# Attention in an attention + mixture-of-experts layer: heads in pairs on row halves, masks of both passes ahead of the scores

## The chip, the cores and the metric

The kernel runs on one core of a Trainium2 chip. The metric is the device time of one execution in microseconds (us). The kernel before takes 1405.36 us, the median of three runs (1402.96 to 1407.62).

## The reference

```python
x = x + attn(layernorm(x))                  # x is 8 x 512 x 256, f32
x = x + experts(layernorm(x))
# attn: q, k, v = x @ W.T + b, 16 heads of 16; rotary embedding on q and k;
#       causal softmax(q k^T / 4) v; then @ Wo.T + bo
# experts: 8 experts, the 2 best of a router for each token, at most 153 tokens
#       per expert and batch; silu((t Wf + bf) * (t Wg + bg)) Wp + bp, weighted sum
```

## The kernel before, in words

The program has two phases, `attention_phase` and `expert_phase`. The diff touches the first. Each of the five engines has its own instruction stream, written out by hand with semaphores between them.

**Slots.** Attention runs over 8 batches (`b`), 4 groups of 4 heads (`g`), and 8 slots (`u`) in each group, on all engines in the same order. A slot is written (g,u). In slot u, TensorE computes two heads' scores twice. The *first pass* (`pass1`, L392) has queries on the partitions, query tile i = u // 2 and 256 to 512 keys; VectorE takes the maximum over the keys (L794). The maxima are transposed (piece M, L465), negated (ScalarE, L584) and sent by DMA as one more row of the query stack (L337). The *second pass* (`pass2`, L412) works on the group of two groups earlier. It has keys on the partitions, key tile j, and 512, 384, 256, 256 queries; the extra row subtracts the maximum, and ScalarE takes the exponential (L569, L577) into `probs`. Then `pv` (L437) multiplies with `v_sb` (L445), its four heads in four column strips of the array; it is called four times per group, at u = 3, 5, 7 and the next group's u = 1.

**Operands.** q and k are split in two parts each (`hilo`), so that fp32r products keep precision. They go to DRAM (L318) and come back (`load_stack`, L320 to 331) as stacks of 4 x 16 rows for a head: all four products of the parts in one matmul of 65 or 66 rows (`qst`, `kst`). The causal mask is added by a matmul with an identity and a bf16 mask: L401/L405 ahead of the first pass's scores, L422/L432 ahead of the second's. Masks and scores of a pass stand together.

**Pieces.** The rest of the work of three batches is cut into pieces, at most one per slot (`PIECES`, L235): for batch b+1 X (transposed normalised input), Q (0 to 3, the projections of q and k, L475) and V (L477); for b A (transposed PV output, L469) and M; for b-1 T and O (output projection, L486 to 491); for b-2 H, L, R, F (router and ranks). All use the PSUM bank `misc`, PV its own; the first pass has four banks, the second two. `last_piece` finds which eviction has to be over before the bank is used again.

**The other engines.** ScalarE evicts Q (L605), X, T, H, PV (L593). VectorE does the reductions, the rotation (shuffle L811, product with sin L812, sum L817), both normalisations (L697), the copy of v (`v_sb`, L822), v's eviction (L774), the residual (L781), attention's scaling (L757, L761) and routing (L703 to L749). POOL does the product with cos (L935), the split of the rotated values (L947, L950), two Newton chains for 1/sqrt (L908 to L916) and the scatter of tokens (L964). SP issues the DMAs. A loop over b = 2 to 6 has the steady code; b = 0, 1, 7, 8 are written out, and the last pieces lie in slots of the experts' first block (`LATE_SLOTS`, L1069).

```python
def pv(t, bt, g, j):                                   # L437
    wait(pe, exp_done, tiles2(t, 2 * j + 1, 1))
...
if u in (3, 5, 7) and (not isinstance(b, int) or 0 <= s - 2 <= 31):
    pv(s - 2, b - (g < 2), (g - 2) % 4, (u - 3) // 2)  # L535
```

Of the kernel before, what the change touches and what calls it, by code (L numbers as in the profile page):

```python
# [6 lines left out]
F32 = mybir.dt.float32  # L7
# [8 lines left out]
P = 128  # L16
BATCH, T, C = 8, 512, 256
TT = T // P
# [5 lines left out]
ZROW = NP * DH  # L24
MROW = ZROW + 1
ROWS = MROW + 1
SLOTS = 8
# [7 lines left out]
MASKED = -1e30  # L35
# [10 lines left out]
CAUSAL = IDENT + P  # L46
# [57 lines left out]
def attention_phase(nc, d, rt, block, outer):  # L104

    ctx = ExitStack()
    with ctx:
# [3 lines left out]
        def sem(name):  # L120
# [11 lines left out]
        ident_bf = sb("ident_bf", [P, P], BF16)  # L132
# [10 lines left out]
        bv_all = sb("bv_all", [P, C])  # L143
# [10 lines left out]
        x1 = late.take("x1", [P, TT, C])  # L154

# [4 lines left out]
        stats1 = sb("stats1", [P, TT, 6])  # L160
        mv1 = sb("mv1", [P, TT, 2])
        rs1 = sb("rs1", [P, 3, TT])
# [8 lines left out]
        qst = sb("qst", [ROWS, NG, GH, T], F32R)  # L171
        kst = sb("kst", [ROWS, NG, GH, T], F32R)
        mx = sb("mx", [P, 2, TT, GH])
        negmax = sb("negmax", [GH, 2, T], F32R)
        probs = sb("probs", [P, 2, GH, T])
        rden = kept.take("rden", [P, TT, GH])
        stats2 = kept.take("stats2", [P, TT, 6])
        mv2 = kept.take("mv2", [P, TT, 2])
        rs2 = kept.take("rs2", [P, 3, TT])
# [19 lines left out]
        pvb = ps[:, 6, :]  # L199
        misc = ps[:, 7, :]  # L200
# [23 lines left out]
        sin_done, rope_done, oh_done, dlt_done, put_done = (sem("sin_done"), sem("rope_done"), sem("oh_done"),  # L224
                                                            sem("dlt_done"), sem("put_done"))
        rs1_done, rs2_done = sem("rs1_done"), sem("rs2_done")
        cos_done, hilo_done, xr_done = sem("cos_done"), sem("hilo_done"), sem("xr_done")
        dve_step, newton1, newton2 = sem("dve_step"), sem("newton1"), sem("newton2")
        hilo_half = sem("hilo_half")
        sp_passed, dve_passed, pool_passed = sem("sp_passed"), sem("dve_passed"), sem("pool_passed")  # L230
# [3 lines left out]

        PIECES = {  # L235
# [7 lines left out]
        }  # L243
        Q_AT = ((1, 1), (1, 4), (1, 6), (2, 1))
        FIRST = [at for at in sorted(PIECES) if PIECES[at][0] in "XQV"]

        def bank_of(b, g, u):
            return ps[:, FIRST.index((g, u)), :] if isinstance(b, int) and b == -1 else misc

        def piece_there(b, g, kind):  # L250
            s = 4 * b + g
            return {
                "M": there(s, 1, 32) if isinstance(b, int) else True,
                "A": there(s, 3, 34) if isinstance(b, int) else True,
# [5 lines left out]
        def freed(b, g, kind, n):  # L260
            return {
                "M": (negmax_out, 4 * b + g),
                "A": (at_out, 4 * b + g - 2),
# [11 lines left out]
        def last_piece(b, g, u):  # L275

            if isinstance(b, int) and b == -1:
                return None
            keys = sorted(PIECES)
            at = keys.index((g, u))  # L280
            for back in range(1, 2 * len(keys)):
# [4 lines left out]
                if (not isinstance(bb, int) or bb >= -1) and piece_there(bb, gg, kind):  # L286
                    if isinstance(bb, int) and bb == -1 and kind not in "XQV":
                        continue
                    return freed(bb, gg, kind, n)
# [1340 lines left out]
```

## Time and profile before

| | us |
|---|---|
| median of three runs | 1405.36 (1402.96 to 1407.62) |
| the profiled execution, its own time | 1391.76 |
| its span | 1389.9 |
| TensorE busy | 1238.5 |
| VectorE busy | 729.6 |
| POOL busy | 697.0 |
| ScalarE busy | 496.3 |
| mean granted TensorE clock | 0.943 |

In the rows below PE is TensorE's matmuls, PEld its weight loads, DVE is VectorE, ACT ScalarE, POOL GpSimd, SP the engine that issues most DMAs; "q" behind a name is an engine's queue. `L401` is line 401. A busy matmul includes its latency; the distance between the starts of two matmuls says what one costs. The granted clock is the share of TensorE's full clock that the chip let it have.

### The profile page before, as it was taken

The page shows a single profiled execution, that of the slowest core. Times are in us where ns is not written, and L with a number is a line of the kernel's source. Part 1 is how long each engine was busy: PE and PEld are TensorE (multiplying, and loading weights), DVE is VectorE, ACT ScalarE, POOL GpSimd, SP SyncE. Part 2 cuts the span into 40 slices and gives each one's busy share as a digit, 9 for nine tenths or more (in the row PEclk, how much of TensorE's full clock was granted, in tenths as well). Part 3 has the DMA queues.
Part 4 walks back from the last instruction along what each step waited for, and adds up shares of the span by engine and source line. Part 5 has one row for each costly group of instructions (what it writes and reads, how often), then busy time and mean ns, then how long its engine had stood idle before and what let it go on. Part 6 is the DMA issues. An engine that isn't in the chain of part 4 may idle for free.

```text
span 1389.9 us, 25801 instructions
## 1 busy us (share of the span) xinstructions
PE 1238.5 (89%) x8360; PEld 1023.6 (74%) x8360; DVE 729.6 (52%) x1512; ACT 496.3 (36%) x988; POOL 697.0 (50%) x984
## 2 busy tenths in 40 slices
PE   3699999999898989988899999999999999997830
PEld 3465656566565656548899999999999999997730
DVE  5777776858676767556333343343333433333336
ACT  2145444535353535454223332333233332332100
POOL 4334243343425251267755665576656764634445
PEclk9699999999999999999999999999999999998865
DMA  5766545444434453432312211131122112102247
GB/s 138 216 208 193 177 115 144 109 132 103 138 93 139 100 149 93 137 124 60 96 62 91 70 62 62 64 98 54 66 78 87 54 58 70 64 28 72 69 131 249
DMA packets 82333, 147.86 MB, mean 106 GB/s; under 512 B 9263, under 2 KB 59832, under 8 KB 78142
## 3 DMA queue, kind: packets, MB, share of 16 engines
q1 hardware_dynamic: 64576, 111.37, 28.1%
q0 software_dynamic: 7936, 26.60, 5.6%
q10 hardware_dynamic: 9728, 8.67, 2.0%
q8 instruction: 56, 0.92, 0.3%
q14 instruction: 37, 0.30, 0.1%
HBM read 93.05 MB, written 53.61 MB: 106 GB/s over the span
## 4 chain that ended last, share of the span: by engine, by line
PE 45%; another core or an unknown queue 2%; DVE 1%; POOL 1%; issue 1%; DMA 0%; DVEq 0%; ACT 0%; POOLq 0%; ACTq 0%
PE ps L77 44%; PE ps L1264 1%; DVE raw L1427 1%; POOL wg_hi L1544 1%; POOL wf_hi L1544 0%; DMA wg_hi<-slot_outputs,slot_all 0%; DVE al L1417 0%; DVEq L1454 0%; DVE ah L1408 0%; POOLq L1572 0%; ACT hid L1349 0%; ACT fc L1360 0%; DVE xl L1332 0%; DVE gated L1455 0%
## 5 line engine op out<-in xcount | busy, mean ns | idle before, releaser
L1491 POOL TENSOR_TENSOR al<-hid,ah 128x384 fp32r<-128x384 f32 (+1 forms) x176 | 187.4, 1065 | 232.9 <-DVE ah L1408 232.9
L1360 ACT ACTIVATE fc<-ps,b_fc 128x384 f32<-128x384 f32 (+1 forms) x192 | 115.5, 602 | 482.4 <-PE ps L77 441.2
L1455 DVE SCALAR_TENSOR_TENSOR gated<-ps,b_gate,fc 128x384 f32<-128x384 f32 (+1 forms) x192 | 123.4, 643 | 268.1 <-PE ps L77 220.2
L794 DVE TENSOR_REDUCE mx<-ps 128x2 f32<-128x256 f32 (+3 forms) x256 | 206.6, 818 | 67.1 <-PE ps L408 56.5
L577 ACT ACTIVATE probs<-ps 128x512 f32<-128x512 f32 (+1 forms) x256 | 125.6, 541 | 73.8 <-PE ps L434 72.0
L408 PE MATMUL ps<-kst,qst 65*128 65x256 f32 (+2 forms) x512 | 151.7, 380 | 0.0
L1442 DVE TENSOR_TENSOR o_sb<-ps,b_proj 128x256 f32<-128x256 f32 x80 | 33.9, 424 | 179.0 <-PE ps L77 175.1
L569 ACT ACTIVATE probs<-ps 128x256 f32<-128x256 f32 (+1 forms) x128 | 62.6, 490 | 164.4 <-PE ps L425 150.0
L445 PE MATMUL ps<-probs,v_sb 128*32 128x512 f32 (+3 forms) x1024 | 98.8, 459 | 14.2 <-DVE v_sb L822 14.0
L77 PE MATMUL ps<-xh,wg_hi 128*128 128x384 f32 (+1 forms) x384 | 104.4, 353 | 5.0 <-DVE gated L1455 4.2
L935 POOL TENSOR_TENSOR rope_c<-qk_b,rope_table 128x512 f32<-128x512 f32 x32 | 42.7, 1333 | 128.9 <-ACT qk_b L605 128.7
L77 PE MATMUL ps<-wp_hi,ah 128*128 128x256 f32 (+1 forms) x640 | 89.7, 283 | 17.0 <-DVE al L1417 17.0
L434 PE MATMUL ps<-qst,kst 66*128 66x512 f32 (+1 forms) x256 | 103.9, 457 | 0.0
L77 PE MATMUL ps<-xh,wg_lo 128*128 128x384 f32 (+1 forms) x384 | 103.8, 352 | 0.0
L77 PE MATMUL ps<-xl,wg_hi 128*128 128x384 f32 (+1 forms) x384 | 103.8, 352 | 0.0
L1349 ACT ACTIVATE hid<-gated 128x384 f32<-128x384 f32 (+1 forms) x192 | 102.8, 535 | 1.4 <-DVE gated L1455 0.8
L77 PE MATMUL ps<-xh,wf 128*128 128x384 f32 (+1 forms) x384 | 90.6, 358 | 7.4 <-DVE xl L1332 7.3
L77 PEld LDWEIGHTS ps<-wp_hi,ah 128*128 128x128 f32 (+1 forms) x640 | 83.3, 186 | 17.9 <-issue 17.6
L77 PE MATMUL ps<-wp_hi,al 128*128 128x256 f32 (+1 forms) x640 | 88.9, 281 | 0.0
L77 PE MATMUL ps<-wp_lo,ah 128*128 128x256 f32 (+1 forms) x640 | 88.6, 281 | 0.0
L1408 DVE CAST ah<-hid 128x384 fp32r<-128x384 f32 (+1 forms) x192 | 87.7, 457 | 0.8 <-ACT hid L1349 0.8
L408 PEld LDWEIGHTS ps<-kst,qst 65*128 65x128 f32 x512 | 83.1, 204 | 2.5 <-issue 0.3
(181 smaller groups left out, 2577.5 us busy)
## 6 DMA issues: line engine op xcount, KB each, us to landing
qk_parts<-hilo SPq DMA_DIRECT2D x32, 512.0 KB, 3.1
qst<-qk_parts SPq DMA_DIRECT2D x64, 256.0 KB, 4.8
kst<-qk_parts SPq DMA_DIRECT2D x64, 256.0 KB, 5.2
slot_tokens<-zeros POOLq DMA_DIRECT2D x12, 816.0 KB, 5.6
rows<-slot_tokens SPq DMA_DIRECT2D x24, 384.0 KB, 3.7
slot_outputs<-o_sb SPq DMA_DIRECT2D x72, 128.0 KB
raw<-in_wf SPq DMA_DIRECT2D x8, 1024.0 KB, 6.1
raw<-in_wg SPq DMA_DIRECT2D x8, 1024.0 KB, 7.6
```

The source lines that it names most:

```text
L77: last = nc.tensor.matmul(out, w, x, start=(i == 0), stop=(i == len(terms) - 1))
L408: last = mm(bank, qst[0:MROW, g, h, bass.ts(i, P)], kst[0:MROW, g, h, 0:width], start=False, stop=True, skip_group_check=True)
L434: mm(ps[:, S2 + hh, 0:T - q0], kst[0:ROWS, g, h, bass.ts(j, P)], qst[0:ROWS, g, h, q0:T], start=False, stop=True, skip_group_check=True).t ...
L445: last = mm(pvb[32 * h:32 * h + 32, P * j:T], v_sb[:, j, GH * g + h, :], probs[:, j % 2, h, P * j:T], start=(j == 0), stop=(j == TT - 1))
L569: A(probs[:, j % 2, 2 * pr:2 * pr + 2, P * j:T], ps[:, S2 + pr, :].rearrange("p (h q) -> p h q", h=2)[:, :, P * j - q0:T - q0], ACT.Exp, s ...
L577: A(probs[:, j % 2, 2 * pr + hh, P * j:T], ps[:, S2 + hh, P * j - q0:T - q0], ACT.Exp, scale=float(DH) ** -0.5).then_inc(exp_done, 1)
L794: V.reduce_max(mx[:, g % 2, i, 2 * pr:2 * pr + 2], both[:, :, 0:P * (i + 1)], AXX)\
L1349: A(hid[:, hc % 2, 0:width], gated[:, hc % 2, 0:width], ACT.Silu).then_inc(hid_done, 1)
L1360: A(fc[:, hc % 2, 0:width], ps[:, FC + hc % 2, 0:width], ACT.Identity, bias=b_fc[:, e, hc:hc + 1]).then_inc(fc_out, 1)
L1408: V.tensor_copy(ah[:, (8 * n + hc) % RING, 0:width], hid[:, hc % 2, 0:width]).then_inc(ah_done, 1)
L1455: V.scalar_tensor_tensor(gated[:, hc % 2, 0:width], ps[:, GATE + hc % 2, 0:width], b_gate[:, e, hc:hc + 1], fc[:, hc % 2, 0:width], ALU.ad ...
L1491: G.tensor_tensor(al[:, at, 0:width], hid[:, hc % 2, 0:width], ah[:, at, 0:width].bitcast(F32), ALU.subtract).then_inc(al_done, 1)
```

## The change

**Row halves.** The stacks keep three products of the parts instead of four: 48 rows and one for the maximum, 49 in all. Heads lie in pairs: one head of a pair in partitions 0 to 48, the other in 64 to 112. Each mask becomes a matmul of 64 rows: `pick_bf` has two entries per row, one of them 2^-88, and the mask has values for two columns of positions, so that 64 rows make 128. Each head of a pair has its own bank, in both passes.

**Order in a slot.** The masks of the first pass, the masks of the second pass, the scores of the first, the scores of the second, the pieces. The second pass's masks wait for the exponentials of the slot before. There is one exponential per slot, for both heads (8 semaphore counts per group instead of 12).

**PV.** One piece "P" at u = 1, for all key tiles of the group before the previous one; `probs` keeps a whole group, packed.

**Pieces.** They use two banks, LOW and HIGH (6 and 7), and a slot can have two: X,X at (0,0); O,O at (3,0). Q moves to (0,4), (0,6), (1,0), (1,5), V to (3,4), (3,5), M to u = 2; L, R, F and the routing move later, the scatter to (2,6), (2,7), (3,0), (3,1).

**Work moved.** POOL now multiplies by cos and sin (`cos_sin`), normalises (both), copies v, and has one Newton chain for both norms. VectorE shuffles the sin product and adds (`rotate`). ScalarE makes the large part of the split (`large_part`) and evicts v; POOL makes the small part. v's bias is folded into the output bias, once, in the prologue. The input of batch b+2 is loaded and normalised in b, one batch earlier. A stack load is eight DMAs instead of four, the row of maxima two instead of one. Batch 6 is written out too. The experts' code is the same, but for wait counts.

```diff
-            def pass2(t, g, u):
-                if u >= PAIRED:
-                    wait(pe, exp_done, tiles2(t, u, 0) - 2)
-                    mm(bank[:, :, P * j - q0:P * (j + 1) - q0], ident_bf[:], later_bf[:].unsqueeze(1).to_broadcast([P, 2, P]),
-                        start=True, stop=False, skip_group_check=True)
...
+            rows_of = [slice(HALF * hh, HALF * (hh + 1)) for hh in range(2)]
+            def first_masks(b, g, u):
+                if u == 0:
+                    wait(pe, ld_stack[g], 128 * (b + 1))
+                wait(pe, red_done, 8 * (4 * b + g) + u - 1)
+                for hh, half in enumerate(rows_of):
+                    mm(first_bank(u, hh)[:, bass.ts(u // 2, P)], pick_bf[half, 0], causal_bf[half],
+                       start=True, stop=False, skip_group_check=True)
+            def first_scores(g, u):
+                for hh in range(2):
+                    rows = slice(HALF * hh, HALF * hh + MROW)
+                    last = mm(first_bank(u, hh)[:, 0:width], qst[rows, g, pr, bass.ts(i, P)], kst[rows, g, pr, 0:width],
+                              start=False, stop=True, skip_group_check=True)
+                last.then_inc(p1_done, 1)
+            def second_masks(t, u):
+                if u == 0:
+                    wait(pe, ld_max, 32 * (t + 1))
+                wait(pe, exp_done, TILES2 * t + u)
...
+                elif kind == "P":
+                    wait(pe, exp_done, TILES2 * (s - 2))
+                    for j in range(TT):
+                        for h in range(GH):
+                            last = mm(misc[32 * h:32 * h + 32, P * j:T], v_sb[:, j, GH * group + h, :],
+                                      probs[:, (g + 1) % 2, h, PROB_AT[j]:PROB_AT[j + 1]], start=(j == 0), stop=(j == TT - 1))
...
+                for g, u in before_late(b):
+                    s = 4 * b + g
+                    if there(b, 0, 7):
+                        first_masks(b, g, u)
+                    if second_there(s):
+                        second_masks(s - 2, u)
+                    if there(b, 0, 7):
+                        first_scores(g, u)
+                    if second_there(s):
+                        second_scores((g - 2) % 4, u)
+                    pieces(b, g, u)
...
+            def exps(t, g, u):
+                wait(act, p2_done, TILES2 * t + u + 1)
+                A(probs[:, g % 2, 2 * pr:2 * pr + 2, PROB_AT[j]:PROB_AT[j + 1]], ps[:, S2:S2 + 2, P * j - q0:T - q0], ACT.Exp,
+                  scale=float(DH) ** -0.5).then_inc(exp_done, 1)
...
+            def large_part(b, n):
+                wait(act, rope_done, 4 * b + 4 + n + 1)
+                wait(act, st_hilo[n // 2], 32 * (b + 1))
+                A(hilo[:, n, 0, :], rope_c[:, n % 2, :], ACT.Copy).then_inc(hilo_half, 1)
+            LARGE_AT = ((1, 0), (1, 2), (1, 4), (2, 3))
...
+            def rotate(chain, b, n):
+                wait_apart(dve, cs_done, 4 * b + 4 + n + 1, dve_passed)
+                chain(V.stream_shuffle(qk_b[:, n % 2, :], rope_s[:, n % 2, :], SWAP))
+                V.tensor_tensor(rope_c[:, n % 2, :], rope_c[:, n % 2, :], qk_b[:, n % 2, :], ALU.add).then_inc(rope_done, 1)
+            ROTATE_AT = ((0, 7), (1, 1), (1, 3), (2, 2))
```

## Rows read from the trace of the kernel before

**Rows 1.** The page, busy time, share of the span and instructions of each engine.
```profile
PE 1238.5 (89%) x8360; PEld 1023.6 (74%) x8360; DVE 729.6 (52%) x1512; ACT 496.3 (36%) x988; POOL 697.0 (50%) x984
```

**Rows 2.** Windows by batch: us, then busy us (instructions) of each engine; last clock, DMA.
```profile
39.80:96.20 56.40, 50.83 (x298) 33.63 (x298) 40.88 (x67) 17.69 (x34) 19.76 (x32) 0.80 0.71 218
162.60:235.30 72.70, 67.69 (x502) 43.77 (x499) 52.52 (x114) 33.34 (x68) 28.36 (x46) 0.95 0.50 136
...
383.20:457.10 73.90, 68.02 (x501) 44.16 (x497) 52.53 (x114) 33.34 (x68) 29.08 (x49) 0.95 0.45 120
...
531.40:592.50 61.10, 57.94 (x445) 36.13 (x441) 36.62 (x82) 29.89 (x62) 14.09 (x26) 0.94 0.45 121
...
626.00:1389.90 763.90, 685.01 (x4415) 664.34 (x4413) 299.94 (x633) 222.78 (x437) 455.05 (x600) 0.95 0.24 79
```

**Rows 3.** Timeline of PE, slot (1,2) of a batch: start, us, instruction.
```profile
403.36 0.28 PE L401 MATMUL ps<-causal_bf,ident_bf 128*128 128x256 bf16 x1
...
404.02 0.23 PE L432 MATMUL ps<-later_bf,ident_bf 128*128 128x128 bf16 x1
404.06 0.42 PE L434 MATMUL ps<-qst,kst 66*128 66x384 f32 x1
404.32 0.28 PE L401 MATMUL ps<-causal_bf,ident_bf 128*128 128x256 bf16 x1
```

**Rows 4.** Timeline of PE, a PV step and a Q projection; groups of lines, both O.
```profile
405.57 1.07 PE L445 MATMUL ps<-probs,v_sb 128*32 128x512 f32 x8
406.57 0.65 PE L451 MATMUL ps<-consts_sb,pv_sb 128*128 128x128 f32 x4
...
412.52 0.62 PE L77 MATMUL ps<-xnT_hi,wq_hi 128*128 128x512 f32 x2
...
413.92 0.28 PE L405 MATMUL ps<-causal_bf,ident_bf 128*128 128x128 bf16 x2
...
L490 PE MATMUL ps<-wo,attnT 128*128 128x256 f32 x16 | 4.0, 392 | 0.0
```

**Rows 5.** Groups of ACT, one batch: busy us, mean ns | idle before, releaser.
```profile
L577 ACT ACTIVATE probs<-ps 128x512 f32<-128x512 f32 x16 | 8.7, 593 | 6.0 <-PE ps L434 5.9
L577 ACT ACTIVATE probs<-ps 128x384 f32<-128x384 f32 x16 | 7.0, 490 | 4.2 <-PE ps L434 4.0
```

**Rows 6.** Groups of DVE, the same batch.
```profile
L794 DVE TENSOR_REDUCE mx<-ps 128x2 f32<-128x1024 f32 x9 | 10.9, 1219 | 3.4 <-remote 1.5 <-issue 1.2 <-PE ps L408 0.7
...
L811 DVE STREAM_SHUFFLE rope_s<-qk_b 128x512 f32<-128x512 f32 x4 | 3.0, 740 | 0.0
...
L741 DVE TENSOR_SCALAR over<-pos 128x8 f32<-128x8 f32 x1 | 1.8, 1776 | 0.0
```

**Rows 7.** Groups of POOL, the same batch.
```profile
L964 POOL DMA_INDIRECT slot_tokens<-hn,put_at x8 | 8.1, 1007 | 3.9 <-issue 2.0 <-DVE put_at L747 1.9
...
L935 POOL TENSOR_TENSOR rope_c<-qk_b,rope_table 128x512 f32<-128x512 f32 x4 | 5.1, 1276 | 17.0 <-ACT qk_b L605 17.0
```

**Rows 8.** Waits of PE in that batch (us, times, longest); PE's first slot, timeline.
```profile
PE ps L445 <- DVE v_sb L822: 2.5, 1, 2.5
...
39.82 0.37 PE L401 MATMUL ps<-causal_bf,ident_bf 128*128 128x256 bf16 x1 [11.98 <-DMA kst<-qk_parts]
```

**Rows 9.** Windows of 4 us: PE, PEld, DVE, ACT, POOL busy, granted clock, DMA.
```profile
40.00:44.00 4.00, 2.79 (x15) 2.16 (x14) 3.02 (x11) 0.00 (x0) 0.81 (x4) 0.50 1.07 275
...
604.00:608.00 4.00, 3.26 (x23) 1.52 (x22) 3.66 (x13) 3.60 (x8) 1.54 (x1) 1.00 0.89 303
...
423.00:427.00 4.00, 2.15 (x10) 0.52 (x11) 2.30 (x4) 0.00 (x0) 3.07 (x3) 0.70 0.25 90
...
403.00:407.00 4.00, 4.00 (x29) 2.14 (x28) 2.99 (x7) 2.41 (x6) 1.27 (x1) 1.00 0.69 162
```

**Rows 10.** Timeline of PE, the A pieces of two groups in the last pass.
```profile
598.75 0.66 PE L451 MATMUL ps<-consts_sb,pv_sb 128*128 128x128 f32 x4
...
609.11 0.66 PE L451 MATMUL ps<-consts_sb,pv_sb 128*128 128x128 f32 x4
```

More of the change, by code:

```diff
@@ L380, in _ @@
             body(1)
-            with sp.Fori(2, 7) as b:
+            with sp.Fori(2, 6) as b:
                 body(b)
-            body(7)
-            body(8)
+            for b in range(6, 9):
+                body(b)
             rt["late_slot"]["sp"] = body_slot
@@ L547, in _ @@
+            pe.wait_ge(bv_ready, 1)
+            for c in range(CK):
+                last = mm(bank_of(-1, "X", 1)[:, 0:C], bv_wide[:, c, :], wo[:, c, :], start=(c == 0), stop=(c == CK - 1))
+            last.then_inc(bo_done, 1)
             pe.wait_ge(made, 5)
             pe.wait_ge(ld_ones, 32)
+            pe.wait_ge(v_out, 2)
+            pe.wait_ge(bo_out, 1)
             body(0)
             body(1)
-            with pe.Fori(2, 7) as b:
+            with pe.Fori(2, 6) as b:
                 body(b)
-            body(7)
@@ L554, in _ @@
-            body(8)
-            rt["late_slot"]["pe"] = piece
+            for b in range(6, 9):
+                body(b)
+            rt["late_slot"]["pe"] = pieces
         @block.scalar
@@ L776, in body_slot @@
-                if (g, u) in ((3, 2), (3, 3)) and piece_there(b, g, "O"):
-                    n = u - 2
-                    wait(dve, o_done, 2 * b - 2 + n + 1)
+                    for n in range(CK):
+                        wait(dve, xT_out, 2 * b + 2 + n + 1)
+                        V.tensor_tensor(xnT[1][:, n, :], bank_of(b, "X", n), xnT[0][:, n, :].bitcast(F32), ALU.subtract)\
+                            .then_inc(xl_out, 1)
+                if (g, u) == (3, 1) and there(b, 1, 8):
                     wait(dve, xr_done, b)
@@ L833, in body @@
+                if (g, u) == (3, 2) and there(b, 1, 8):
+                    wait(dve, o_out, 2 * b)
+                    layer_stats(chain, x1, 1, mv2_done)
             def body(b):
@@ new lines, in rsqrt, with normalise, normalise_input @@
+                    step(G.tensor_tensor(y, y, a, ALU.mult))
+            def normalise(dst, src, which, done):
+                for k in range(TT):
+                    ins = G.tensor_scalar(dst[:, k, :], src[:, k, :], mv[:, which, k, 0:1], rs[:, 1, which, k:k + 1],
+                                          ALU.subtract, ALU.mult)
+                ins.then_inc(done, 1)
+            def normalise_input(b):
+                wait_apart(pool, xT_done, 2 * b, pool_passed)
+                normalise(xn, x_in, 0, xn_done)
@@ L955, in body_slot @@
                         .then_inc(xr_done, 1)
+                if (g, u) == (2, 3) and there(b, 0, 7):
+                    wait(pool, v_out, 2 * (b + 1))
+                    wait_apart(pool, pv_done, 4 * b, pool_passed)
+                    G.tensor_copy(v_sb[:, :, :, 0:DH], v_next[:].rearrange("p t (h r) -> p t h r", h=HEADS)).then_inc(v_moved, 1)
                 if (g, u) in SCATTER_AT and there(b, 2, 9):
@@ L992, in _ @@
             pool.wait_ge(st_zero, 16 * FILLS)
-            with pool.Fori(2, 7) as b:
+            with pool.Fori(2, 6) as b:
                 body(b)
-            body(7)
-            body(8)
+            for b in range(6, 9):
+                body(b)
             rt["late_slot"]["pool"] = body_slot
@@ L1619 @@
         "consts": constants(),
-        "rows": np.stack([np.zeros(NG * GH * T, np.float32), np.ones(NG * GH * T, np.float32)]),
+        "ones": np.ones((1, NG * PAIRS * T), np.float32),
     }
```

608 lines of the change are left out of this document (280 added, 328 removed), and 7 rows, old and new, of the table PIECES.

## The prediction

> **What bounds the kernel now.** I read the page first, for the stages [rows 1]: TensorE is busy 89% of the span, VectorE 52%, POOL 50%, ScalarE 36%. The change touches only the attention phase, so the windows by batch come next [rows 2]. A batch in the loop takes 72.7 us at its start and 73.9 in the middle, with TensorE busy 68.0 and VectorE 52.5. The last full batch, which prepares no successor, takes 61.1. After 626 us only experts are left, some 764 us that the diff leaves alone.
>
> The timeline of TensorE inside one batch says what a slot costs [rows 3]. A slot without a piece runs from 403.36 to 404.32: 0.96 us for 256+512 columns of the first pass and 2 x (128+384) of the second. The granted clock is 1.00 there, the 2.4 GHz level (403 to 407 has it throughout [rows 9]), at which 1792 columns are 0.75 us; the other 0.21 is loading of weights and hand-overs. So the plain slot is TensorE's own work. Thirty-two of them are 31 us. The pieces, by their starts [rows 4]: 1.00 us for a PV step of 512 columns (2.5 for the 1280 of a group), 1.40 for a Q projection, 2.0 for each half of O (4.0 busy for both); V has Q's columns. 4 x 2.5 + 4 x 1.4 + 2 x 1.5 + 2 x 2.0 = 22.6 us, and 17 short ones at some 0.5 make 31. That is 62 of 74 us. Most of the other 12 is stalls in group 2, as the wait for v_sb (2.5 us) [rows 8], and what follows them at the half clock, as 423 to 427 with 0.70 [rows 9].
>
> **The change, step by step.**
>
> *Masks and scores on row halves.* Two heads now lie in partitions 0-63 and 64-127, and the matmuls of each pair name different halves and different banks. If a pair streams together, a slot's columns fall from 1792 to 128+128+256+384 = 896, 0.37 us. Loads stay, eight for seven; what they and the hand-overs cost is the 0.21 us of the plain slot [rows 3], and I take 0.3 for more waits between changes of weights. The slot is 0.7 us of TensorE work in place of 0.96. The trace shows no row halves; it shows the other direction, PV's four heads in column strips, 8 matmuls of 512 columns in 1.07 us, where 0.21 us each in turn would be 1.7 at the least [rows 4]. That is the nearest row and I take full overlap; no overlap is the other end.
>
> Row halves alternate with the full array wherever a slot has a piece. The PV step now starts 0.3 us or so after the last scores and the next work starts about 0.1 after its stream; I take 0.1 us for a change of shape, with 0 and 0.2 as bounds. The Trainium skill (TensorEngine Tiling (Array Packing), Key Properties) says that different tiles run in parallel and also that a change of tiling mode drains TensorE. By that rule alone 23 slots with pieces, entered and left, would be charged; with 0.2 us for each such slot it is 4.6 us a batch, against 16 PV calls in shape changes before.
>
> *The new loop.* Exp of a pair is now one activation over two banks, and the second pass's masks wait for the exp of the slot before; behind that wait on TensorE are this slot's first scores, so VectorE waits too. ScalarE's exps cost 490 and 593 ns for 384 and 512 elements, 0.80 ns an element more [rows 5]. Pairs have 1024, 768, 512, 256: 1.00, 0.80, 0.59, 0.39 us. From the second mask's load to the end of its score is 0.46 us (404.02 to 404.48) [rows 3]; the first scores in between add 0.15, two hand-overs 0.2. So the loop is exp + 0.8: 1.8, 1.6, 1.4, 1.2 us for the four row blocks, twice each: 12.0 us a group, 48 a batch. That is above TensorE's 0.7. The old slot let the second head's matmul run beside the first head's exp.
>
> *Pieces fill the loop.* A piece runs while the exp does, so a slot lasts the larger of the loop and 0.8 + piece. PV is one piece for 1280 columns: 1280/512 x 1.00 = 2.5 us (bounds 2.3, its streams, and 2.7, the sum of the four steps now). Its slot is 3.3, 1.5 over the loop, four times: 6.0. Four Q (2.2 us slots) add 3.0, two V 1.6, the two O together (0.8 + 4.0) 3.0. Transposes and the router's pieces are within the loop. 48 + 13.6 = 61.6 us, about what it is now without stalls.
>
> *VectorE, ScalarE, POOL.* VectorE loses the sine product, both normalisations, the move of v and v's eviction. It keeps the reduction, 1.22 us in slots 6 and 7 [rows 6], as long as those slots. A rotation (0.74 for its shuffle, about as much for the sum [rows 6]) sits behind a reduction, and ScalarE's large part waits for it, one slot later, ahead of that slot's exp. The rotation of slot (0,7) ends 1.5 us into (1,0); the exp is late by some 1 us. The same at (1,4) and (2,3): 3.3 us a batch. In group 2, slots 4 to 7, VectorE has some 0.7 of attention output, reductions of 2 x 0.9 + 2 x 1.22, and some 4 of routing (one step alone is 1.78) [rows 6]: 9 us in 5.3 us of slots. Two banks and the long slot (3,0) behind it take up part; I take 2.5 us of stall. The old stalls on v_sb and attnT lose their causes, as the move is POOL's at (2,3) and PV of that group is read only in the next group.
> POOL gains 4 sine products at 1.28 [rows 7], eight normalisations (no more than 0.64 each, half a product's elements) and the v copy, and loses 4 conversions and half of the Newton steps: 29 us [rows 2] become about 38 of 68. Its scatters (8.1 us and gaps of 3.9 [rows 7]) start at (2,6) and end near (3,3); the Newton chain and the normalisation follow and end some 1.5 us ahead of the X piece at (0,0). I charge 1 us. A full batch is 61.6 + 3.3 + 2.5 + 1 = 68.4 us.
>
> *DMA.* A stack load is eight transfers instead of four, with 48 rows per head for 64. Per group it has eight slots, over 12 us, to land; hidden, except for the first: body 0 starts on kst, after a wait of 11.98 us [rows 8]. There the four more transfers, POOL's normalisation and the later rotation all count; I take a quarter of that wait, +3 us (bounds 0 and 6).
>
> *The ends.* Body 7: 61.1 -> 58.5 (loop, P, O and the routing stall remain). Bodies 0 and 1 took 56.4 and 66.4 (96.2 to 162.6) [rows 2]; I give them 4.4 each. Body 8 has no first pass; its groups took 10.4 us each (598.75 to 609.11 [rows 10]), and the loop (exp + 0.65) with the single PV piece makes them 12.4: +4.
>
> Sum: 5 x (73.9 - 68.4) = 27.5, + 2.6, + 8.8, - 4, - 3: **32 us saved.** The profiled execution took 1391.8 us for a span of 1389.9; the three runs shown have a median of 1405.4, 1% above it, and I subtract from the median: **1373 us**.
>
> **The rivals.**
> *A, the stalls are not there* (0.20). If VectorE keeps ahead, so that rotations and routing hide, a batch is 61 to 63 us: 5 x 12 + 8 for body 7 + 12 - 7 = 73 us saved, **1332**. For it: the LARGE_AT slots leave one to two slots to each rotation. Against it: reductions as long as the slots.
> *B, the clock falls* (0.11). The loop leaves TensorE waiting in a third of the batch. Where the granted clock is 0.50, work doubles. At 40 to 44 us TensorE, with first passes alone, was busy 2.79 of 4 us and stayed at 0.50, the 1.2 GHz level; at 604 to 608 it was busy 3.26 of 4 with second passes and pieces, and had 1.00 [rows 9]. The second is like the new slots, so this is unlikely. Its place is slots (1,6) to (2,0) and (2,4) to (2,7), and what follows them. If the mean granted clock of a batch falls from 0.95 to about 0.80, that is 40% of the time at half; of 55 us of TensorE work 14 to 20 more, half of it beside waits: +8 us a batch, more than 5.5. Then **1413**, slower. It decides once the mean is under 0.85.
> *C, row halves do not overlap* (0.06). Then a slot has 1664 to 1792 columns again, the loop grows by 0.35 to 0.4: +12 a batch, 80 us, and 1373 + 12 x 7.5 is **1463**. Against it: the column strips of rows 4.
> *D, one more queue* (0.06): POOL's chain misses the X piece by 4 us a batch, or ScalarE's evictions push each exp: the gain is about 30 less, **1402**.
>
> **How the numbers follow.** The forecast has 0.57. About 0.3% (4 us) is what a measurement of this kernel can tell from no change. Faster: 0.57 + 0.20 and a bit of D and B, 0.79. Same: 0.06. Slower: the rest of B and C, 0.15. The unknown costs (overlap of loads 0.1 x 32, shape changes 0 to 4.6, PV 0.2 x 4 per batch) are +-4 us a batch, +-25 in all. The range reaches from A's 1332 to the edge of no change, 1330 to 1404; B's and C's slower ends and some of A's lower side are the 0.2 left out.
>
> **What would show it.** Rows of a first pair of score matmuls with starts a few ns apart and 0.35 us or less from the first mask to the second mask's load; plain slots of 1.2 to 1.8 us, ended by exp; PV in one group of 32 matmuls near 2.5 us; a batch of 66 to 70 us between two v copies; VectorE near 65% of a batch; ScalarE idle ahead of hilo behind rope_c in (1,0), (1,4), (2,3). Wrong would be score pairs with starts 0.1 us or more apart (C), a mean clock under 0.85 in the middle batches (B), or TensorE waiting at X for xn (D).

## The result, and the profile of the changed kernel

Four runs of the changed kernel have a median of 1522.4 us (1511.8 to 1526.2), four of the kernel before 1404.2 (1400.9 to 1407.6): a ratio of **1.083**, 95% interval 1.077 to 1.089. The forecast was 1373 us. The kernel became 8.3% slower, and the time lies above every case that was written down. Some executions of a kernel are over 1.5% longer than its fastest; ratios leave them out and medians do not, so a ratio can differ a little from the quotient of two medians.

The page of the changed kernel, busy time and share of each engine, then the granted clock in 40 slices:

```profile
span 1524.3 us, 25626 instructions
...
PE 1222.9 (80%) x8620; PEld 981.1 (64%) x8620; DVE 660.3 (43%) x1398; ACT 513.8 (34%) x904; POOL 786.6 (52%) x986
...
PEclk9557777787878889887879999999999999999965
```

TensorE's busy time hardly fell against [rows 1], and its share went from 89% to 80%: the added time is waiting. The windows by batch (us, busy time of PE, PEld, DVE, ACT, POOL, granted clock, DMA share, GB/s):

```profile
49.80:138.60 88.80, 43.57 (x282) 26.27 (x284) 32.87 (x54) 19.49 (x29) 29.63 (x39) 0.62 0.35 127
...
309.30:393.00 83.70, 66.26 (x532) 38.38 (x533) 43.66 (x98) 35.74 (x58) 39.77 (x44) 0.82 0.28 94
393.00:479.60 86.60, 66.23 (x530) 38.73 (x529) 43.48 (x98) 35.82 (x58) 39.75 (x44) 0.80 0.28 91
```

A batch takes 84 to 87 us where [rows 2] had 73 to 74, and the first 88.8 where it had 56.4. The busy share of the 16 DMA engines fell from 0.45 to 0.28 in the middle batches, so on average they have time to spare. The slots themselves came out as planned. The timeline of the changed kernel in one slot with the M piece:

```profile
405.48 0.23 PE L395 MATMUL ps<-causal_bf,pick_bf 64*128 64x128 bf16 x2
...
405.54 0.22 PE L414 MATMUL ps<-later_bf,pick_bf 64*128 64x128 bf16 x2
...
405.57 0.36 PE L403 MATMUL ps<-kst,qst 48*128 48x256 f32 x2
...
405.77 0.34 PE L422 MATMUL ps<-qst,kst 49*128 49x384 f32 x2
...
406.05 0.60 PE L442 MATMUL ps<-consts_sb,mx 128*4 128x128 f32 x4
```

From the first masks to the start of the M piece are 0.57 us, with a pair of 256 columns in 0.36 us and one of 384 in 0.34. The granted clock is 1.00 there, at which the 1792 columns of rival C would be 0.75 us by the prediction's sum and 896 are 0.37. So the row halves stream together, and rival C is out. The other 0.20 us is what the plain slot before had too (0.21 [rows 3]): a cost of the change to the full array, which M brings, can't be seen in this slot. What is lost is lost between slots.

Long waits between 120 and 680 us (us in all, times, longest), and single rows of the timeline:

```profile
DVE mx L796 <- PE ps L403: 156.3, 112, 4.7
POOL xr L933 <- DMA xr<-in_x: 104.0, 7, 28.7
ACT probs L564 <- PE ps L422: 95.4, 140, 5.7
...
ACT hilo L582 <- DVE rope_c L756: 55.7, 18, 9.8
```

```profile
49.86 0.29 PE L395 MATMUL ps<-causal_bf,pick_bf 64*128 64x128 bf16 x2 [17.83 <-DMA kst<-qk_parts]
...
73.62 2.44 SPq L321 DMA_DIRECT2D kst<-qk_parts  x1
...
79.53 2.46 SPq L321 DMA_DIRECT2D kst<-qk_parts  x1
82.03 0.58 SPq L301 DMA_DIRECT2D x_in<-in_x  x1
...
92.60 1.41 DVE L688 BATCH_NORM_STATS2 stats<-x_in 128x6 f32<-128x256 f32 x4 [34.55 <-DMA x_in<-in_x]
...
95.32 0.29 PE L395 MATMUL ps<-causal_bf,pick_bf 64*128 64x128 bf16 x2 [33.20 <-DVE mx L796]
...
407.25 0.40 SPq L347 DMA_DIRECT2D xr<-in_x  x1
...
417.57 2.37 POOL L933 TENSOR_TENSOR xr<-xr,bo_all 128x1024 f32<-128x1024 f32 x1 [13.38 <-DMA xr<-in_x]
...
422.59 0.72 DVE L755 STREAM_SHUFFLE qk_b<-rope_s 128x512 f32<-128x512 f32 x1
...
424.30 0.63 ACT L582 ACTIVATE hilo<-rope_c 128x512 fp32r<-128x512 f32 x1 [8.19 <-DVE rope_c L756]
...
425.89 0.29 PE L414 MATMUL ps<-later_bf,pick_bf 64*128 64x128 bf16 x2 [3.79 <-ACT probs L564]
```

There are two places, and stack loads stand ahead of both. At the start SP is held at its own issues of stack loads until 82 us: single ones take 2.4 to 4.5 us, where in the kernel before they take 0.6 to 0.9. So x_in comes late and TensorE stands still for 33.2 us. In a later batch, shown here, the load of xr goes out at 407.25, right behind the eight transfers of a stack load, and lands at 417.57. POOL waits for it, cos_sin of the rotation stands behind POOL's wait, the rotation behind cos_sin, ScalarE's large part behind the rotation, the exp behind that, and TensorE's second masks behind the exp. For a stack itself TensorE's matmuls wait only 8.2 us in all, seven times, between 120 and 680 us. The page's table of issues gives the load of xr a median of 10.5 us from issue to landing; in the kernel before it is 4.8.

Why is a stack load slow when the DMA share is low? In lines 317 and 319 the source of a 32-row load walks the hi/lo copy first, 2 steps, and then 16 channels; in the kernel before, the channels came first, 16 steps. In a stretch where almost nothing but stack loads is moved the share is small (us, five engines' busy time, clock, DMA share, GB/s):

```profile
72.00:76.00 4.00, 0.00 (x0) 0.00 (x0) 0.00 (x0) 0.00 (x0) 0.00 (x0) 0.50 0.18 62
```

A share of 0.18 is 2.9 of 16 engines, with a short burst of a 16-row load in it; from 72.0 to 73.6 us and from 74.4 to 76.0, around the burst, it is 0.13, which is two engines. While the old loads ran, the share was 1.07 [rows 9]. **Theory 1** is that the first dimension of these loads sets how many DMA engines share them, two here. The Trainium skill (DMA: Bandwidth & Descriptors, Why a DMA increments its semaphore by 16 and not by 1) states such a rule: the number of engines is the largest up to 16 that divides the slowest dimension of both sides, 2 for these loads and 16 for the old ones. The rivals: the new order of work makes the stalls (**2**); the clock does, 0.87 in place of 0.94 (**3**); runs of 2048 bytes, or more issues, make the loads slow (**4**).

### The profile page after: what moved, and what is told of

The parts are those of the page before. It is cut to its first block and busy times, and to the rows that moved or that the text cites. A ratio compares the mean times of both kernels' runs of the same rounds, so it can differ in the third digit from the quotient of the medians.

```text
span 1524.3 us, 25626 instructions
## 1 busy us (share of the span) xinstructions
PE 1222.9 (80%) x8620; PEld 981.1 (64%) x8620; DVE 660.3 (43%) x1398; ACT 513.8 (34%) x904; POOL 786.6 (52%) x986
## 5 line engine op out<-in xcount | busy, mean ns | idle before, releaser
L564 ACT ACTIVATE probs<-ps 128x1024 f32<-128x1024 f32 (+3 forms) x256 | 179.7, 702 | 166.9 <-PE ps L422 121.5
L414 PE MATMUL ps<-later_bf,pick_bf 64*128 64x128 bf16 x512 | 62.0, 238 | 96.8 <-ACT probs L564 86.1
L451 PE MATMUL ps<-probs,v_sb 128*32 128x512 f32 (+3 forms) x1024 | 110.0, 579 | 10.4 <-DVE x L785 8.5
L403 PE MATMUL ps<-kst,qst 48*128 48x256 f32 (+2 forms) x512 | 118.1, 458 | 0.0
L395 PE MATMUL ps<-causal_bf,pick_bf 64*128 64x128 bf16 x512 | 62.5, 240 | 67.6 <-DVE mx L796 38.5
L395 PEld LDWEIGHTS ps<-causal_bf,pick_bf 64*128 64x128 bf16 x512 | 25.9, 96 | 129.9 <-issue 65.9
L414 PEld LDWEIGHTS ps<-later_bf,pick_bf 64*128 64x128 bf16 x512 | 26.0, 96 | 122.3 <-ACT probs L564 103.0
L960 POOL DMA_INDIRECT slot_tokens<-hn,put_at x64 | 63.7, 995 | 70.9 <-DVE put_at L747 53.8
L80 PE MATMUL ps<-xh,wf 128*128 128x384 f32 (+1 forms) x384 | 90.2, 357 | 8.0 <-issue 5.1
L422 PE MATMUL ps<-qst,kst 49*128 49x256 f32 (+2 forms) x512 | 95.6, 368 | 0.0
```

The source lines that it names most:

```text
L80: last = nc.tensor.matmul(out, w, x, start=(i == 0), stop=(i == len(terms) - 1))
L395: mm(first_bank(u, hh)[:, bass.ts(u // 2, P)], pick_bf[half, 0], causal_bf[half], start=True, stop=False, skip_group_check=True)
L403: last = mm(first_bank(u, hh)[:, 0:width], qst[rows, g, pr, bass.ts(i, P)], kst[rows, g, pr, 0:width], start=False, stop=True, skip_group_ ...
L414: mm(ps[:, S2 + hh, P * j - q0:P * (j + 1) - q0], pick_bf[half, 1], later_bf[half], start=True, stop=False, skip_group_check=True)
L422: last = mm(ps[:, S2 + hh, 0:T - q0], kst[rows, g, pr, bass.ts(j, P)], qst[rows, g, pr, q0:T], start=False, stop=True, skip_group_check=True)
L451: last = mm(misc[32 * h:32 * h + 32, P * j:T], v_sb[:, j, GH * group + h, :], probs[:, (g + 1) % 2, h, PROB_AT[j]:PROB_AT[j + 1]], start=( ...
```

## The experiments

### Who slows the stack load: e1 to e4

Four kernels on one chip, where the kernel before takes 1403.9 us. The changed kernel was not run there; its row below is the first measurement, beside a kernel before of 1404.2 us.

**e1**: channels first. So that a row stays one run, the weights' channel order puts the two heads of a row half side by side (the diff shows q; k, its broadcast and the 16-row loads follow).

```
-    return a.reshape(*a.shape[:-1], NG, GH, DH).swapaxes(-1, -2).reshape(a.shape)
+    return np.moveaxis(a.reshape(*a.shape[:-1], NG, PAIRS, 2, DH), (-1, -2, -3), (-3, -2, -1)).reshape(a.shape)
-                    q = rt["qk"][b, 0, :, group, :].rearrange("c (d p h) t -> h c d p t", p=PAIRS, h=2)[hh]
+                    q = rt["qk"][b, 0, :, group, :].rearrange("c (d h m) t -> h d c (m t)", h=2, m=PAIRS)[hh]
```

> The changed kernel with the order of the stack load's rows turned round: the 32-row loads walk source and destination by channel first (16 steps) and by the hi/lo copy second, and the channel order inside a group puts the two heads of a row half side by side, so that a row is one run of 4096 bytes. Theory 1 (the stack loads are slow because the 32-row ones run on two DMA engines): their packets spread over all engines, the stretches with two busy engines go, the wait of POOL for xr (104.0 us in the attention) falls under 30, the batches come to 55 to 68 us, and the time to 1310 to 1390 us. Theory 2 (the new order of the work makes the stalls: masks ahead, the rotation's chain): no change, 1490 to 1530. Theory 3 (the clock is the cause): the same as theory 2, with the granted clock still near 0.87.

**e2**: the same with `h c d (m t)`, so runs of 4096 bytes, but two steps first.

> As the run before in channel order and in runs of 4096 bytes, but the 32-row loads walk the hi/lo copy first (2 steps), as in the changed kernel. Theory 1 (two DMA engines): the packets are twice as long and half as many, and still go over two engines: 1470 to 1530 us. Theory 4 (the loads are slow because their packets are of 2048 bytes): as fast as the run before, 1310 to 1390.

**e3**: the changed kernel's layout and runs, each 32-row load split in two.

```
+                    for i in range(3):
+                        row = HALF * hh + DH * i
+                        sp.dma_start(qst[row:row + DH, g].bitcast(F32), q[i % 2]).then_inc(ld_stack[g], 16)
+                        sp.dma_start(kst[row:row + DH, g].bitcast(F32), k[i // 2]).then_inc(ld_stack[g], 16)
```

> The changed kernel with each 32-row load split into two of 16 rows: twelve issues for a stack load instead of eight, packets of 2048 bytes as in the changed kernel, and every one of them walks 16 channels first. Theory 1 (two DMA engines): 1310 to 1400 us. Theory 4 (packets of 2048 bytes, or too many issues on SP): no better than the changed kernel, 1500 to 1560.

**e4**: the kernel before with its loads turned the other way (the diff shows q; k likewise).

```
-                    q = rt["qk"][b, 0, :, group, :].rearrange("c (d h) t -> d c (h t)", h=GH)
+                    q = rt["qk"][b, 0, :, group, :].rearrange("c (d h) t -> c d (h t)", h=GH)
```

> The kernel before with one edit: its stack loads walk the hi/lo copy first (2 steps) and the channels second; bytes, issues and runs of 8192 bytes stay as they are. Theory 1: the 1.05 MB of a stack load go over two DMA engines and take 20 us or more where a group of the kernel before has 18: 1480 to 1900 us. Theories 2, 3 and 4: no change, 1400 to 1410.

| kernel | first steps | run, bytes | issues | xr lands after, us | time, us | ratio (95%) |
|---|---|---|---|---|---|---|
| before | 16 | 8192 | 4 | 4.8 | 1403.9 | 1 |
| changed | 2 | 2048 | 8 | 10.5 | 1522.4 | 1.083 (1.077 to 1.089) |
| e1 | 16 | 4096 | 8 | 3.9 | 1441.8 | 1.033 (1.022 to 1.044) |
| e2 | 2 | 4096 | 8 | 10.8 | 1518.5 | 1.084 (1.070 to 1.099) |
| e3 | 16 | 2048 | 12 | 4.0 | 1476.0 | 1.057 (1.044 to 1.070) |
| e4 | 2 | 8192 | 4 | 17.4 | 1634.2 | 1.168 (1.156 to 1.180) |

With 16 first steps xr lands after 3.9 to 4.8 us, with 2 after 10.5 to 17.4, over a factor of four in run length and in both kernels. e4 is the plainest: the old kernel, same bytes, same issues, the first two dimensions of the sources of q and k exchanged, 16.8% slower. In e4 all loads of a stack are of that kind, in the changed kernel four of eight, which may be why xr lands later still.

The packets say the same. The pages count them, here for the kernel before, e4, the changed kernel, e1 and e3:

```profile
DMA packets 82333, 147.86 MB, mean 106 GB/s; under 512 B 9263, under 2 KB 59832, under 8 KB 78142
...
DMA packets 80541, 147.85 MB, mean 90 GB/s; under 512 B 7471, under 2 KB 58040, under 8 KB 76350
...
DMA packets 90942, 139.59 MB, mean 92 GB/s; under 512 B 9777, under 2 KB 60250, under 8 KB 90832
...
DMA packets 86591, 139.60 MB, mean 97 GB/s; under 512 B 11570, under 2 KB 62043, under 8 KB 86481
...
DMA packets 94783, 139.61 MB, mean 95 GB/s; under 512 B 13617, under 2 KB 64090, under 8 KB 94672
```

Under 512 bytes e4 has 1792 fewer than the kernel before, and e1 1793 more than the changed kernel: 14 for each of the 128 loads of 32 rows, as if such a load had 16 small packets in place of 2. e3 has 256 loads of 16 rows in their place and 3840 more than the changed kernel, again 16 each.

Theory 1 holds; by these counts and by the share of 0.13 the trace agrees with the rule of the Trainium skill. The trace has no numbers of the single DMA engines. Theories 2 and 3 fail as explanations of this part. As the cause of the late xr the run length is out too (e2). The number of issues has a price of its own: e3 is 34 us above e1 with twelve issues for eight, and its runs are also shorter; which of the two it is was not separated. But e1 came to 1442 and not to the 1310 to 1390 expected, and e3 to 1476, between the ranges of theories 1 and 4, so something else is wrong with my sum.

Where the 81 us from the changed kernel to e1 lie: the first copy of v (`v_sb`) starts at 111.4 us in the one and at 81.3 in the other, so 30 us are gone in the first body, where x_in comes late. The rest falls in the later batches.

### What is left: e5 to e8

Edits on e1, on a second chip (kernel before 1393.0 us). In e1 a batch takes 76 us, and its timeline shows POOL's normalisation ahead of the X piece, and what TensorE does behind the wait:

```profile
331.61 4.86 POOL L901 TENSOR_SCALAR xn<-x_in,mv,rs 128x256 f32<-128x256 f32 x4 [0.38 <-POOL rs L897]
...
336.52 1.97 PE L429 MATMUL ps<-consts_sb,xn 128*128 128x128 f32 x8 [3.53 <-POOL xn L901]
...
339.50 3.91 PE L452 MATMUL ps<-probs,v_sb 128*32 128x512 f32 x32
```

**e5**: both normalisations back on VectorE, at (3,7).

```
-                    normalise_input(b + 2)
...
+                if (g, u) == (3, 7) and there(b, 0, 5):
+                    wait_apart(dve, newton, 14 * (b + 3), dve_passed)
+                    wait_apart(dve, xT_done, 2 * (b + 2), dve_passed)
+                    normalise(xn, x_in, 0, xn_done)
```

> The version with sixteen-step loads and rows of 4096 bytes, and the two layer normalisations of a batch back on VectorE (both at slot (3,7)); POOL keeps the Newton chain. In that version POOL takes 4.86 us for the four activations' worth of xn and 4.83 for hn, and TensorE waits 3.5 us ahead of the X piece for xn. Theory A (this wait, and the half clock of 336 to 344 us behind it, are a large part of what is left over the forecast): the wait falls under 1.5 us, a batch of 76 us comes to 70 to 72, and the time to 1400 to 1415. Theory B (VectorE cannot take 3.4 us more a batch, its reductions come late): no change or up to 1455.

**e6**: each pass's masks ahead of its own scores.

```
-                    if second_there(s):
-                        second_masks(s - 2, u)
                     if there(b, 0, 7):
                         first_scores(g, u)
+                    if second_there(s):
+                        second_masks(s - 2, u)
```

> The version with sixteen-step loads, with each pass's masks right ahead of its own scores: first masks, first scores, second masks, second scores. The wait of the second masks for the exp then no longer holds the first scores. Theory C (masks ahead cost: VectorE's reduction starts late by the wait for the exp, 0.3 to 0.9 us in a plain slot): the wait of TensorE on ScalarE stays but the reduction starts earlier, and a batch loses 2 to 6 us: 1400 to 1430. Theory D (the exp sets the plain slot, whatever lies ahead of it): within 1% of 1442.

**e7**: both.

> The two edits before together. If they act on different slots, their gains add: with theories A and C 1365 to 1400, with A alone 1400 to 1415, with neither about 1442.

**e8**: 16 matmuls of 512 columns that nobody reads, where TensorE waits for xn.

> The version with sixteen-step loads, with 16 matmuls of 512 columns of bfloat16 that nobody reads put ahead of TensorE's wait for xn at the X piece (about 3.5 us at full clock, where TensorE waits 3.5 to 3.8 us now). They leave out nothing. Theory E (the half clock behind the wait is a price of its own): the granted clock behind the X piece stays near 1.00, the X piece falls from 1.97 to about 1.0 us and the P piece from 3.9 to about 2.5, and a batch loses 1.5 to 2.5 us: 1420 to 1435. Theory F (only the wait counts; the clock would not be held, or the pieces are waited for elsewhere anyway): 1440 to 1460.

| kernel | time, us | ratio (95%) | last v copy, us |
|---|---|---|---|
| before | 1393.0 | 1 | 561.8 |
| e1 (on its chip) | 1441.8 | 1.033 (1.022 to 1.044) | 592.6 |
| e5, VectorE normalises | 1433.5 | 1.034 (1.027 to 1.041) | 579.9 |
| e6, own masks | 1398.3 | 1.004 (0.999 to 1.009) | 563.3 |
| e7, both | 1393.9 | 1.004 (1.000 to 1.008) | 547.0 |
| e8, filled wait | 1436.9 | 1.036 (1.029 to 1.042) | 588.5 |

The last column is the start of the last copy of v, at (2,3) of body 7, in the profiled run (for the kernel before the one that the rows ahead of the prediction come from). The profiled run of e6 took 1408.3 us, 10 above its median, and that of e5, 1423.6, was the fastest of its six.

**The order of the masks costs 3%** (1.033 to 1.004 from e1 to e6, on two chips; on one chip 1433.5 to 1393.9 us, 39.6 less, from e5 to e7, which differ by this edit alone). The exps of two slots of 512 elements, in e1 and then in e6 (start, us; in brackets ScalarE's idle time before and its releaser):

```profile
381.91 0.60 ACT L565 ACTIVATE probs<-ps 128x512 f32<-128x512 f32 x1 [0.68 <-PE ps L423]
...
383.19 0.60 ACT L565 ACTIVATE probs<-ps 128x512 f32<-128x512 f32 x1 [0.68 <-PE ps L423]
```

```profile
361.72 0.60 ACT L565 ACTIVATE probs<-ps 128x512 f32<-128x512 f32 x1 [0.50 <-PE ps L423]
...
362.82 0.60 ACT L565 ACTIVATE probs<-ps 128x512 f32<-128x512 f32 x1 [0.50 <-PE ps L423]
```

From exp to exp it is exp + 0.68 with the masks of both passes ahead, and exp + 0.50 with each beside its scores (e5 and e7 have the same two values for 512 elements): the first scores stood between the second masks and the second scores, inside the loop. In the other order they run while the exp does. VectorE's waits for the first scores fall too, from 118.9 to 103.3 us between 100 and 560 us. 32 times 0.18 would be 5.8 us a batch, but not every slot has this gap: between v copies e1 takes 75.4 to 77.9 us in the loop and e6 71.3 to 74.8, some 3 us less (e5 to e7: 3.5).

**POOL's normalisation** costs 4 us a batch (e5: 70.3 to 74.1 between v copies): TensorE's wait for xn goes from 3.5 to 1.4 us, as theory A had it. But the whole time of e5 shows no such gain; expected were 1400 to 1415 us. Why the ratio stayed is open; the trace of e5 is 12 us shorter than that of e1, the medians 8, and the kernel before is 11 us faster on the chip of e5. From e6 to e7, the same edit on one chip, the medians differ by 4 us while the last v copy comes 16 us earlier.

**The clock** was held by e8. Behind the filled wait, from its timeline and its windows:

```profile
333.17 3.63 PE L461 MATMUL ps<-tri_bf 128*128 128x512 bf16 x16
...
336.73 1.09 PE L429 MATMUL ps<-consts_sb,xn 128*128 128x128 f32 x8
...
338.79 2.36 PE L452 MATMUL ps<-probs,v_sb 128*32 128x512 f32 x32 [0.35 <-DVE xnT_lo L782]
```

```profile
336.00:340.00 4.00, 3.65 (x33) 1.83 (x35) 1.62 (x3) 2.08 (x3) 4.00 (x4) 1.00 0.37 113
```

In e1 the windows 336 to 340 and 340 to 344 have 0.50 and 0.67 granted, the 1.2 GHz level for a good part; here it is 1.00, the 2.4 GHz level. X falls from 1.97 to 1.09 us and P from 3.91 to 2.36, as expected. The batch gains 0.5 to 1 us of those 2.4. The kernel gains nothing that can be seen: its 1436.9 us lie between the ranges of theories E and F, and its ratio is 1.036 beside 1.033 for e1. That speaks for theory F: at this place the half clock behind a wait mostly fills time in which others are waited for.

### The last batch, and xr once more: e9 to e12

In e7 the v copies come 15 us earlier than in the kernel before, and the kernel is no faster. The trace has the reason in the stage that I had left alone: in the first expert TensorE waits for hn of the last batch (the late H piece). **e9** moves one entry of the table of late slots:

```
-    "dve": {-2: ((8, 2, 4),), -1: ((8, 3, 1), (8, 3, 2), (8, 2, 5), (8, 2, 6)),
+    "dve": {-2: ((8, 2, 4), (8, 2, 5)), -1: ((8, 3, 1), (8, 3, 2), (8, 2, 6)),
```

> The version with sixteen-step loads, normalisations on VectorE and each pass's masks beside its own scores, with one entry of the table of late slots moved: VectorE's slot (8,2,5), which makes the last batch's scatter addresses, goes ahead of (8,3,1) and (8,3,2) and of the split of the first experts' input. Theory T (TensorE's one wait of 14.5 us for hn in the first expert is POOL's queue: scatters, then Newton steps, then hn; the scatters wait for the addresses): the wait falls to 0 to 5 us, and the time by 8 to 13: 1380 to 1386. Theory U (the wait moves to the next late piece): 1390 to 1396.

**e10** is the changed kernel with each pass's masks beside its own scores, **e12** the changed kernel with xr loaded at (3,5) of the body before, and **e11** is e9 with that edit of e12:

```
-                if (g, u) == (0, 1) and there(b, 1, 8):
-                    wait(sp, o_out, 2 * (b - 1))
+                if (g, u) == (3, 5) and there(b, 0, 7):
+                    wait(sp, o_out, 2 * b)
```

> The changed kernel as it is (two-step loads), with one edit: each pass's masks right ahead of its own scores. On sixteen-step loads this took 1442 to 1398 us. Theory C (the first scores behind the wait for the exp cost in every slot): 1475 to 1495. Theory G (with slow loads the slots wait for something else, so the order costs less): 1500 to 1525.

> The changed kernel with one edit: the load of xr is issued at slot (3,5) of the body before, after the stack load of (3,0), instead of at (0,1) right behind the eight transfers of the stack load of (0,0). Theory 1a (the slow stack load does its harm mainly through xr, for which POOL waits 104 us in the attention while cos_sin, rotation, large part and Q stand behind it): this wait falls under 40 us, and the time to 1470 to 1495. Theory 1b (other waits, as those for kst and for ScalarE behind group 3's load, take its place): over 1505.

> The run before with the load of xr at (3,5) as well. POOL still waits 14 us twice in 80 for xr in that version. If cos_sin stands behind that wait and TensorE behind cos_sin, a batch loses 1 to 3 us: 1365 to 1382. If the wait is covered, no difference (within 4 us).

They ran on a third chip, where the kernel before takes 1341.5 us: e9 1347.0 (ratio 1.005, 1.002 to 1.008), e10 1463.7 (1.092), e12 1444.2 (1.076), e11 1364.7 (1.010, 1.006 to 1.015). The times can't be set beside the earlier ones, and the changed kernel had not run there. Only e11 against e9 can be read: by the ratios xr early gives nothing once the loads are fast, and rather costs. It shows one thing more. In e9 POOL waits 105.9 us in all for xr between 120 and 640 us, more than the 90.5 of the changed kernel, though xr lands after 4.0 us; in e11 this wait is 4.3, and the kernel is no faster. So the length of POOL's wait does not say what the transfer costs; the time from issue to landing and the edit that moves it do.

The rest was repeated side by side, on a fourth chip.

> The kernel before once more, unedited, for its trace on the same chip as the three runs beside it. The runs behind e10 stood beside a kernel before of 1341 us where earlier ones stood beside 1393 to 1404. If the difference is the chip's, in the experts' end, the attention phase (last v copy at 561.8 us) and the first expert (86.4 us) stay within 1% and only the stretch behind the seventh expert moves; if it goes through the attention phase too, times of e9 to e12 cannot be set beside those of e1 to e8.

> The changed kernel once more, unedited, beside the kernel before: ratio 1.08 to 1.115. With it stands or falls what e10 (1.0917) and e12 (1.0760) showed.

> e12 again (xr loaded at (3,5) of the body before), beside the changed kernel on one chip. Theory 1a (the slow load acts mainly through xr): the batches of 82 to 88 us come to 75, which is 40 to 60 us under the changed kernel. Theory 1b: within 20 us of it.

> e10 again (each pass's masks beside its own scores), beside the changed kernel on one chip. Theory C (the order costs whatever the loads do): 25 to 45 us under the changed kernel. Theory G (slow loads cover it): 0 to 15 us under it.

The kernel before that stands beside these four takes 1402.7 us.

| kernel, one chip | time, us | ratio (95%) | last v copy, us |
|---|---|---|---|
| r13, before | 1400.4 | 0.997 (0.992 to 1.002) | 561.1 |
| r14, changed | 1520.0 | 1.083 (1.075 to 1.092) | 677.8 |
| r15, xr loaded early | 1483.7 | 1.057 (1.049 to 1.065) | 632.9 |
| r16, own masks | 1500.2 | 1.070 (1.060 to 1.079) | 653.7 |

With xr out of the stack load's way POOL's wait for it goes from 90.5 us (r14, same window) to one of 14.2 (r15, 120 to 640 us):

```profile
POOL rope_c L912 <- ACT qk_b L577: 57.5, 24, 7.4
...
POOL xr L933 <- DMA xr<-in_x: 14.2, 1, 14.2
```

The time falls by 36 us, just under the 40 to 60 expected: more than a third of what the loads cost (81 us, changed to e1) acted through this one transfer. The first v copy is still at 111.3 us, so the 30 us of the first body are not among them. The masks' order is worth 20 us here, between the two expectations: the slow loads cover half of its 40.

The last pair, on a fifth chip (kernel before 1340.3):

> e7 again (sixteen-step loads, normalisations on VectorE, masks beside their own scores), beside e9 on one chip. Its ratio to the kernel before was 1.004; the same is expected.

> e9 again (e7 with the last batch's scatter addresses made ahead), beside e7 on one chip. Theory T (TensorE's wait of 14.5 us for hn in the first expert was the queue of POOL behind late addresses): 8 to 13 us under e7, ratio to the kernel before 0.993 to 0.998. Theory U (the wait only moves): within 3 us of e7.

r17 took 1354.5 us (1.011, 1.008 to 1.015), r18 1345.8 (1.005, 1.003 to 1.007): 8.7 us less, as theory T has it, though not the ratio of 0.993 to 0.998 that was expected with it, as r17 itself came out at 1.011 where e7 had 1.004. TensorE's wait, in r17 and then in r18:

```profile
621.21 1.09 PE L429 MATMUL ps<-consts_sb,hn 128*128 128x128 f32 x4 [14.47 <-DVE hn L699]
```

```profile
626.97 1.08 PE L429 MATMUL ps<-consts_sb,hn 128*128 128x128 f32 x4 [5.47 <-DVE hn L699]
```

No version beat the kernel before. r18 is its equal within half a per cent, on the slow side.

## Why the prediction was wrong

**Row halves overlap: right.** 0.57 us for both passes of a slot, 0.7 charged. The PV piece takes 2.36 us at the full clock (e8), 2.5 charged. Two counts are off without weight: `PIECES` has 26 slots with pieces and not 23, and rival C's 12 us a batch are 90 us in its sum and not 80.

**The loop: exp + 0.8: measured exp + 0.68** behind 512 elements, and up to 0.81 for exps of 1024. The form was right and the size a little high. What I missed is that the same sentence held a loss: I wrote that the first scores stand behind the wait for the exp, priced the slot with them inside, and never asked what the slot would be with them outside. The price of the order that the change is named for is some 40 us on fast loads (e5 to e7).

**"A stack load is eight transfers instead of four", with "eight slots, over 12 us, to land; hidden, except for the first": this step failed.** I priced a load by its bytes and issues and did not read the order of its dimensions. The loads of 32 rows ran on two DMA engines (share 0.13, two small packets for a load). From the changed kernel to e1 that is 81 us, where the sum had 3. The first load cost TensorE a wait of 17.8 us where [rows 8] had 11.98, which is 6 more and at the edge of my bound; but SP's queue behind it held x_in, and that wait is 33.2 us. The step also looked only at who waits for the stacks, and that wait is indeed small in the later batches (8.2 us in all); the transfers behind them on the queue were hit harder: r15 recovers 36 us by moving xr alone.

**POOL: a normalisation at "no more than 0.64 each": 1.22 measured** (4.86 us for four), because I took half a product's elements for half its time, across a different operation. The chain then missed X by 3.5 us, which is rival D's mechanism at its price of 4; with the normalisations on VectorE and the masks in the other order the batches are 67.8 to 71.3 us, and the forecast for a batch was 68.4.

**"After 626 us only experts are left ... that the diff leaves alone": false.** The diff edits `LATE_SLOTS`, the table that puts the last pieces into the experts' first block, so the words in "The change" that the experts' code is the same hold for the experts' own code alone. In e7 the stretch from the last v copy to the first gated product takes 74.2 us in place of 68.3, near the +4 charged, and the first expert (24 such products) 100.2 in place of 86.4. In the changed kernel it is 99.7. These 14 us stood in no term; VectorE makes the addresses of the last scatters 11.6 us after it has their input (608.5 to 620.1 in e7; 611.6 to 616.4 in the kernel before), POOL's Newton steps stand behind the scatters, and hn behind those. e9 and r18, which make these addresses earlier, have 88.6 and 90.2 us for the first expert. The same traces say why e7 is no faster than the kernel before: its last v copy comes 14.7 us earlier, then it takes 5.9 us more to the first gated product and 13.8 more for the first expert.

**Rival B, the clock.** Its sign was met (0.79 to 0.84 in the middle batches, under 0.85), but as a consequence: e4 has 0.73 in a batch of the old kernel with slow loads, and e8 holds the clock at one wait for no gain. How much of the loss the lower clock itself adds was not separated.

So of 149 us between 1373 and 1522 the runs account for 81 by the loads and some 40 by the order of the masks; 14 more are the first expert. The overlap of these with each other (20 us for the order where loads are slow) is why such a list is no exact sum. The 14 us are read from traces: the edit on them (r17 to r18) gave 8.7, and some 10 us of the 149 stay open.

## What to carry to other kernels

For each transfer that a change rewrites, read the order of its dimensions as well as its bytes, and then list what is queued behind it: here a falling DMA share together with late landings meant few engines at work. Judge a transfer by its time from issue to landing, and not by how long an engine waits for it. When a sum ends with "the rest is left alone", look up every table in the diff that places work in the rest. A loop between two engines should be priced in both orders of its independent work.

## What the runs showed that I had not expected

Two dimensions exchanged in the sources of q and k, with bytes, runs and issues the same, took xr's landing from 4.8 to 17.4 us and the old kernel from 1404 to 1634 us (e4). The kernel before took 1393 to 1404 us on three chips and 1340 to 1341 on two others; from the 168th to the 192nd gated product of the experts it is 112 us in r14, on one of the three, and 84 in r17, on one of the two, so a good part of the difference sits there. Its cause was not looked into.
